# A sparse expert layer's prologue: router as two diagonal blocks, sums over tiles by one scan

## What is computed

```python
flat = x.reshape(-1, C)
logits = flat @ router_w.T
probs = jax.nn.softmax(logits, axis=-1)
topk_probs, topk_idx = jax.lax.top_k(probs, TOP_K)
topk_probs = topk_probs / (jnp.sum(topk_probs, axis=-1, keepdims=True) + 1e-09)
h1 = jnp.einsum('nc,ehc->neh', flat, w1)
h3 = jnp.einsum('nc,ehc->neh', flat, w3)
h = jax.nn.silu(h1) * h3
y = jnp.einsum('neh,ech->nec', h, w2)
out = jnp.einsum('ne,nec->nc', gates, y)
```

## Time and profile before

| | us |
|---|---|
| median of 3 runs (2287.74 to 2291.01) | 2289.25 |
| the profiled execution, its own time | 2279.4 |
| its span, first to last instruction | 2277.6 |
| prologue of ffn2 in that span | 1186.6 to 1268.6 |
| prologue of ffn3 in that span | 1790.2 to 1871.1 |

### The profile page before, as it was taken

One profiled execution on the slowest core, in us unless ns is written; L12 is line 12 of the kernel. 1 busy time (PEld: TensorE's weight loads), 2 busy tenths in 40 slices (PEclk: granted clock), 3 DMA queues, 4 the chain that ended last, 5 costly groups with the idle time before them and its releaser, 6 DMA issues. The chain is left out here.

```text
span 2277.6 us, 30440 instructions
## 1 busy us (share of the span) xinstructions
PE 1677.3 (74%) x11157; PEld 967.5 (42%) x11157; DVE 1245.0 (55%) x2416; ACT 965.8 (42%) x1715; POOL 590.1 (26%) x591
## 2 busy tenths in 40 slices
PE   2899996897999970312304599999845539999994
PEld 2433333345333340100103366666545426666663
DVE  6643335655633357578787555555462565555554
ACT  2565653333655543325123244444322424444441
POOL 0100000001000000000005577743452157776332
PEclk8899997996999975556555799999967759999997
DMA  1322210002222200000000354444268014544444
GB/s 41 76 68 65 65 56 20 0 0 50 76 65 65 65 23 0 0 0 0 0 4 27 117 147 147 149 138 134 92 152 167 7 57 149 147 146 143 133 133 151
DMA packets 117333, 175.30 MB, mean 77 GB/s; under 512 B 38106, under 2 KB 66522, under 8 KB 116674
## 3 DMA queue, kind: packets, MB, share of 16 engines
q1 hardware_dynamic: 99906, 155.38, 23.8%
q0 software_dynamic: 17280, 17.99, 2.4%
HBM read 148.60 MB, written 24.70 MB: 76 GB/s over the span
## 5 line engine op out<-in xcount | busy, mean ns | idle before, releaser
L1350 DVE TENSOR_TENSOR ffn_hidden<-ffn_silu,ffn_up_ps 114x512 f32<-114x512 f32 x426 | 293.0, 688 | 349.9 <-ACT ffn_silu L1320 349.0
L1262 PE MATMUL ffn_up_ps<-ffn_turned,ffn_weights 64*114 64x256 f32 x3408 | 445.8, 394 | 5.8 <-DMA ffn_weights<-in_ffn_weights 4.9
L1320 ACT ACTIVATE ffn_silu<-ffn_up_ps 114x512 f32<-114x512 f32 x426 | 254.4, 597 | 388.9 <-PE ffn_up_ps L1262 386.5
L826 POOL DMA_INDIRECT slots<-ffn_rows,ffn_slot x256 | 251.7, 983 | 557.4 <-DVE ffn_slot L944 386.4
L736 ACT ACTIVATE ffn_hidden<-ffn_up_ps,ffn_b 128x512 f32<-128x512 f32 x512 | 310.1, 689 | 198.0 <-PE ffn_up_ps L631 198.0
L1241 POOL DMA_INDIRECT results<-ffn_yout,ffn_xin x284 | 271.9, 957 | 246.0 <-DVE ffn_yout L1338 179.6
L1262 PEld LDWEIGHTS ffn_up_ps<-ffn_turned,ffn_weights 64*114 64x114 f32 x3408 | 288.1, 176 | 110.6 <-issue 59.6
L631 PE MATMUL ffn_up_ps<-ffn_T,ffn_up_w 64*128 64x512 f32 x1024 | 261.2, 623 | 3.1 <-ACT ffn_hidden L736 3.1
L652 PE MATMUL ffn_y_ps<-ffn_hidden,ffn_down 128*64 128x512 f32 x1024 | 247.9, 605 | 3.4 <-DVE ffn_y_total L526 3.4
L1273 PE MATMUL ffn_y_ps<-ffn_hidden,ffn_weights 114*64 114x256 f32 x1704 | 215.2, 388 | 0.0
L526 DVE SCALAR_TENSOR_TENSOR ffn_gated<-ffn_y_ps,ffn_b,ffn_gates 128x512 f32<-128x512 f32 x96 | 72.0, 751 | 204.7 <-PE ffn_y_ps L652 203.1
(11 more groups left out here) (412 smaller groups left out, 2067.1 us busy)
## 6 DMA issues: line engine op xcount, KB each, us to landing
ffn_weights<-in_ffn_weights SPq DMA_DIRECT2D x142, 534.0 KB
ffn_gates<-gate_rows SPq DMA_DIRECT2D x128, 256.0 KB
ffn_xin<-slots SPq DMA_DIRECT2D x142, 66.0 KB
sht_mix<-in_sht_weights SPq DMA_DIRECT2D x8, 1024.0 KB, 8.4
results<-ffn_yout,ffn_xin POOLq DMA_INDIRECT x284
slots<-ffn_rows,ffn_slot POOLq DMA_INDIRECT x256
D<-results SPq DMA_DIRECT2D x16, 256.0 KB, 5.4
ffn_second<-results SPq DMA_DIRECT2D x16, 256.0 KB, 5.9
```

The lines of the kernel that those rows point to most:

```text
L826: nc.gpsimd.indirect_dma_start(k.slots, bass.IndirectOffsetOnAxis(slot[c][:, t:t + 1], 0), rows[c][:, t, :], None).then_inc(row_stored[h], 16)
L1262: last = nc.tensor.matmul(up_ps[w][n % 2][0:SIZE, chunk % 2 * BLOCK:(chunk % 2 + 1) * BLOCK], weights[rows_of, b % WEIGHTS, chunk * SIZE:( ...
L1320: nc.scalar.activation(silu[0:SIZE, n % 2, :], up_ps[0][n % 2][0:SIZE, :], ACT.Silu).then_inc(silu_done, 1)
L1350: nc.vector.tensor_tensor(hidden[0:SIZE, b % 2, c, :], silu[0:SIZE, n % 2, :], up_ps[1][n % 2][0:SIZE, :], ALU.mult).then_inc(hidden_done, 1)
```

## The change

The router matrix gets a layout of two diagonal blocks, [128, 16]: the rows of the even tile's channels have the weights in columns 0 to 7 and zeros in 8 to 15, those of the odd tile's the other way round. One product over 128 partitions then gives both tiles' logits side by side, and one copy takes them out. The sums over the tiles are made by one `tensor_tensor_scan`, state = goes_on * state + adds, over a layout in which the tiles of an expert lie next to each other; `goes_on` is 1, and 0 at each expert's first tile. The six other stages are untouched.

```diff
-        self.run = [sb(f"run{i}", [P, TILES + 32, E]) for i in (0, 1)]
+        self.adds, self.until = (sb(n, [P, E * TILES]) for n in ("adds", "until"))
+        self.goes_on = [sb(f"goes_on{h}", [P, E * (t1 - t0)]) for h, (t0, t1) in enumerate(RANGES)]
...
-            small_ps = [[psi(f"small_ps{h}{half}", [P, 512]) for half in (0, 1)] for h in (0, 1)]
+            small_ps = [psi(f"small_ps{h}", [P, PAIRS_OF_TILES, 2, E]) for h in (0, 1)]
...
-                    for half in (0, 1):
-                        product = small_ps[h][half][:, t0 // 2 * E:t1 // 2 * E].rearrange("p (t e) -> p t e", e=E)
-                        ch.link(nc.vector.tensor_copy(r.L[:, t0 + half:t1:2, :], product))
+                    ch.link(nc.vector.tensor_copy(r.L[:, t0:t1, :].rearrange("p t e -> p (t e)"),
+                                                  small_ps[h][:, t0 // 2:t1 // 2, :, :]
+                                                  .rearrange("p i h e -> p (i h e)")))
...
-                    ch.link(nc.vector.tensor_copy(r.run[0][:, 32, :], first))
-                    ch.link(nc.vector.tensor_copy(r.run[0][:, 33:32 + n, :], totals[:, 0:n - 1, :]))
-                    i, step = 0, 1
-                    while step < n:
-                        a, b = r.run[i], r.run[1 - i]
-                        ch.link(nc.vector.tensor_tensor(b[:, 32:32 + n, :], a[:, 32:32 + n, :],
-                                                        a[:, 32 - step:32 + n - step, :], ALU.add))
-                        i, step = 1 - i, 2 * step
-                    until = r.run[i]
-                    ch.link(nc.vector.tensor_tensor(pl, until[:, 32:32 + n, :], before, ALU.add))
+                    adds, until = (x[:, 0:E * n].rearrange("p (e t) -> p t e", e=E) for x in (r.adds, r.until))
+                    ch.link(nc.vector.tensor_copy(adds[:, 0, :], first))
+                    ch.link(nc.vector.tensor_copy(adds[:, 1:n, :], totals[:, 0:n - 1, :]))
+                    ch.link(nc.vector.tensor_tensor_scan(r.until[:, 0:E * n], r.goes_on[h][:, :], r.adds[:, 0:E * n],
+                                                         0.0, ALU.mult, ALU.add))
+                    ch.link(nc.vector.tensor_tensor(pl, until, before, ALU.add))
...
-                for run in r.run:
-                    ch.link(nc.vector.memset(run[:, 0:32, :], 0.0))
+                for h, (t0, t1) in enumerate(RANGES):
+                    ch.link(nc.vector.memset(r.goes_on[h][:, :], 1.0))
+                    ch.link(nc.vector.memset(r.goes_on[h][:, 0:E * (t1 - t0):t1 - t0], 0.0))
...
-                for half in (0, 1):
-                    sp.dma_start(router[half * CH:(half + 1) * CH, :], dram[f"{name}_router"])\
-                        .then_inc(router_loaded, 16)
+                sp.dma_start(router[:, :], dram[f"{name}_router"]).then_inc(router_loaded, 16)
...
-                        for half in (0, 1):
-                            rows_of = slice(half * CH, (half + 1) * CH)
-                            last = nc.tensor.matmul(small_ps[h][half][:, pair * E:(pair + 1) * E],
-                                                    ring[rows_of, g % 2, i * P:(i + 1) * P], router[rows_of, :],
-                                                    start=True, stop=True)
+                        last = nc.tensor.matmul(small_ps[h][:, pair, :, :].rearrange("p h e -> p (h e)"),
+                                                ring[:, g % 2, i * P:(i + 1) * P], router[:, :],
+                                                start=True, stop=True)
```

More of the change, by code:

```diff
@@ L840, in sparse_stage @@
             ring = sbi("ring", [P, 2, NTOK])
-            router = sbi("router", [P, E])
+            router = sbi("router", [P, 2 * E])
             below, ones = sbi("below", [P, P]), sbi("ones", [P, P])
@@ L944, in place @@
                         ch.link(nc.vector.tensor_copy(slot[c][:, t0:t1], r.mark[:, t0:t1]), f"slots{h}{c}")
-                    ch.link(nc.vector.tensor_tensor(r.ends[:, :], until[:, 31 + n, :], totals[:, n - 1, :], ALU.add))
+                    ch.link(nc.vector.tensor_tensor(r.ends[:, :], until[:, n - 1, :], totals[:, n - 1, :], ALU.add))
                     if h == 0:
@@ L949, in place @@
                         ch.link(nc.vector.tensor_copy(pad_slot[:, :], r.ends[:, :]), "ends")
-                        ch.link(nc.vector.tensor_tensor(r.counts[:, 1, :], until[:, 32 + LANDED[1][1] - t0, :], region,
+                        ch.link(nc.vector.tensor_tensor(r.counts[:, 1, :], until[:, LANDED[1][1] - t0, :], region,
                                                         ALU.subtract))
@@ L1080, in counts @@
                         .then_inc(placed, 1)
-                pe.wait_ge(router_loaded, 32)
+                pe.wait_ge(router_loaded, 16)
                 pe.wait_ge(below_loaded, 16)
@@ L3180, in lay_out @@
     for n, src in (("ffn2", "L2_ffn"), ("ffn3", "L3_ffn")):
-        a[f"{n}_router"] = np.asarray(i[f"{src}_router_w"]).T
+        a[f"{n}_router"] = np.zeros((P, 2 * E), np.float32)
+        for half in (0, 1):
+            a[f"{n}_router"][half * CH:(half + 1) * CH, half * E:(half + 1) * E] = np.asarray(i[f"{src}_router_w"]).T
         w = np.zeros((E, P, WEIGHT_COLS), np.float32)
```

## The result

The changed kernel takes 2282.63 us (median of 13 runs, 2271.35 to 2286.0) against 2289.25 for the kernel before on the same chip. The ratio is 0.9972, 95% interval 0.996 to 0.9984: between 3.7 and 9.2 us less. The forecast was 2280.6 with a range of 2276.0 to 2285.5: 2.0 us too low, and the measured time is inside the range. One of the 13 runs of the kernel before took 7328.6 us, for no reason that the record shows; without it the median of the others is 2288.67. The profiled execution takes 2271.35 us against 2279.4, its span is 2269.5 against 2277.6.

What follows compares the result with a forecast made beforehand. VectorE's chain in the prologue was taken to set the second block's start. First range -0.70 and second -3.61 us gave -4.3 us a stage, -8.6 for both: 2289.25 to 2280.6 us, range 2276.0 to 2285.5.

Steps and rivals of the forecast that it cites:

- Memsets and logits' copy, first range: VectorE, first range: new memsets add 0.26 us with nothing hiding them; one logits' copy for two saves 0.20 us.
- Scan: VectorE, both ranges: two steps of 1.06 ns an element, 0.46 and 1.00 us, replacing additions of 1.30 and 3.58 us.
- Rivals 2 and 4: Dear scan: at 6.25 ns an element 2284.8 us, chance 0.11; at 20 ns the kernel is slower, 2298.9 us, chance 0.03.
- Reading across: VectorE's addition behind the scan reads with a step: 0.66 ns more an element, +0.08 us first range, +0.25 second.
- First scatter: GpSimd's first scatter in each stage comes earlier by the first range's saving of 0.70 us.
- rival 1: Router product on TensorE halves, passes staying at 0.107 us: -7.9 us a stage, 2273.5 us; chance 0.05.
- Turn 4: TensorE, second range: start of product 2 to end of turn 4, 2.92 us before, gets 0.1 us shorter.
- turn 5 to the end of product 7: TensorE, second range: 10.34 us becomes 9.2, with 0.1 allowed for the start after a wait: -1.0 us.
- The copy of the second range's logits: VectorE reaches this copy earlier by the first range's 0.70 us and by 1.1 us from TensorE.
- rival 3: Something other than VectorE's chain ends the prologue, so the second block starts no earlier: no change, 2289.25 us; chance 0.05.
- the copies that write `adds` across: VectorE, both ranges: scattered writes cost nothing; 0.66 ns an element, +0.3 us a stage, kept for the range.

Runs made afterwards that it cites:

- masks_on_gpsimd: Changed kernel with goes_on, starts, passed and ones set by GpSimd in place of VectorE; prologues 0.64 us shorter than the changed kernel's.
- by_expert: Changed kernel with TensorE's counting products reading S with a step, so VectorE's copy is straight; prologues 78.08 and 76.82 us against 78.03 and 76.80.
- router_only: Kernel before with the new router product and its one copy, but the doubling additions kept; prologues 1.58 and 1.69 us shorter than the kernel before.
- scan_only: Kernel before with the scan in place of the additions, router left in two halves; prologues 2.27 and 2.43 us shorter than the kernel before.
- halves_in_turn: Kernel before with all even tiles of a group multiplied first, then all odd ones; 0.42% slower, prologues 4.40 and 4.37 us longer.

## Why the prediction was right

It put -4.3 us on each prologue and the measurement is -3.94 and -4.11. Term by term, in ffn2, each read against the load of the router:

- Memsets and logits' copy, first range: the copy starts 0.28 us later (forecast 0.26). They were on the path, as said; masks_on_gpsimd took them off and gained.
- Scan: 0.42 and 0.96 us with 128 and 384 elements (forecast 0.43 and 0.97). Two steps of 1.06 ns for an element were right: (957 - 424) / 256 = 2.08 ns between the two sizes. The Trainium skill (DVE: opcode table, instruction layouts, handler registers and perf-mode slots, section Datapath and trigger behaviour) has it at half throughput, and the trace agrees: 2.08 against the addition's 1.06. Rivals 2 and 4, the dear scan, fall.
- Reading across: 0.37 for 0.29 and 0.80 for 0.56 (L940, in a fence below), as forecast.
- First scatter: -0.60 (forecast -0.70). Of the missing 0.10, 0.08 is the copy at L934, 0.36 where it was 0.28, and 0.02 the memsets.
- TensorE: the passes at 0.213 us, not at 0.107, so the product gains nothing and rival 1 falls. Turn 4 0.11 us quicker (1217.87 to 1220.68, 2.81 for 2.92; forecast 0.1), turn 5 to the end of product 7 in 9.25 for 10.34 (forecast -1.0, measured -1.09). The copy of the second range's logits starts at 48.99 us for 50.78: -1.79, forecast -1.8.
- The end of the prologue still sets the start of the second block, so rival 3 falls.

What the sum lacked, two terms. The first is the copies that write `adds` across, **costed at nothing**, with 0.3 us a stage kept for the range: 0.787 us where the straight copy takes 0.550 (by_expert), and 0.36 where it takes 0.28. That is 0.32 us a stage and 0.63 ns an element, near the 0.66 ns that L985 gave for reading. (L985's own numbers give 0.65.) The row that bounded it was there, and I took the low end. The second is not in the forecast at all: one instruction of 128x8 elements, L957, takes 0.41 us in place of 0.17, once in each stage. VectorE by line and shape:

```profile
L957 DVE TENSOR_SCALAR ffn_counts<-ffn_counts 128x8 f32<-128x8 f32 x6 | 1.5, 248 | 0.2
```

Four of the six take 0.17, so two take 0.41. It does in all five profiles that have both halves of the change, and in none of router_only, scan_only, halves_in_turn and the kernel before. In the kernel before another instruction of this kind is the long one, L917 with 0.38 (scan_only has it too, as L918, and router_only in ffn3), which takes 0.19 elsewhere. The two rows of L896 that begin the fence are for the sum below it:

```profile
1239.38 0.62 DVE L896 TENSOR_TENSOR ffn_marked<-ffn_marked,ffn_consts 128x384 f32<-128x384 f32 x1
...
1243.58 0.59 DVE L896 TENSOR_TENSOR ffn_marked<-ffn_marked,ffn_consts 128x384 f32<-128x384 f32 x1
...
1247.05 0.38 DVE L917 TENSOR_SCALAR ffn_total<-ffn_total 128x48 f32<-128x48 f32 x1
...
1249.28 0.17 DVE L931 COPY ffn_run<-ffn_ends 128x8 f32<-128x8 f32 x1 [0.83 <-PE ffn_before_ps L1079]
...
1253.65 0.56 DVE L940 TENSOR_TENSOR ffn_place<-ffn_run,ffn_before_ps 128x384 f32<-128x384 f32 x1
```

L917 lies ahead of a wait for TensorE and cost nothing; the wait grew by 0.19 (0.83 to 1.02) when it was gone. L957 has no wait behind it, and so 0.24 us are lost. -4.3 + 0.32 + 0.24 = -3.74, and the measurement is -3.94. The 0.2 us between are two things in about equal parts: TensorE gave 1.20 where 1.1 was forecast, and L896 (L897 in the changed kernel) takes 0.62 and 0.59 us in the kernel before and 0.56 twice in the changed one. That second part is luck: both long ones start within 0.03 us of a scatter's start (1239.41 and 1243.58).

What makes the short instructions long was not tested, but the nine traces narrow it down. GpSimd's scatters mostly take 0.96 us. Every TENSOR_SCALAR, CAST or COPY in the prologues from SBUF to SBUF (where all tiles but the `_ps` ones lie) that starts 0.52 to 0.69 us after the start of a scatter is long, 19 of 19, and each ends 0.93 to 0.95 us after that start, when the scatter is nearly over. The same L918 that starts 0.48 us after one keeps its 0.19 us. Instructions with two inputs, reductions, reciprocals and copies out of PSUM that start in that stretch keep their length (L908, 48 elements with two inputs, 0.21 us at 0.54). So it looks as if these kinds wait for the end of the scatter; that is argued from coincidence in time. It means that whatever moves VectorE against GpSimd decides which instruction is hit: L917 in the kernel before, L941 in scan_only, L957 in the changed kernel.

Of the median's miss of 2.0 us, 0.6 is in the prologues (8.6 forecast, 8.05 measured). The remaining 1.4 lies within the interval of the measurement: the saving of 8.05 is inside 3.7 to 9.2, and the second measurement of the same kernel, 0.9966, is 7.8 us.

## What to carry to other kernels

Before two half-height products are merged into one, look at the order of the passes: where they already alternate between the row halves, a merged pass takes twice as long as a half one, and what is gained lies at the seams and in the number of copies. A doubling sum of four or six passes over a few hundred elements is worth a scan at two addition steps an element, and the order it wants costs 0.63 to 0.75 ns for each element wherever one of the instructions has to cross it. Read the gain of such an edit in the stretch that it touches: the stretch repeated within 0.04 us where the start of ffn2 moved by 8 us between two executions of one kernel.

## What the runs showed of the hardware that was not expected

- In the same-half order two streams of passes, one for each row half, run side by side at 0.213 us each, so that 16 passes take 2.75 us and not 3.4. In the second block two column halves over the same rows do the same (L1273). The pace belongs to the part of the array that passes share, not to the array.
- A product whose moving operand is read with a step of 8 elements is slower: 1.73 us for 1.65 with 384 columns.
- A short TENSOR_SCALAR, CAST or COPY within SBUF that starts 0.52 to 0.69 us after the start of one of GpSimd's scatters ends only 0.93 to 0.95 us after it, in 19 of 19 cases: 8 elements take 0.41 us in place of 0.17. The cause is open.
